# One score product per query tile for the query tiles with one or two key blocks: all four heads of a group in one pair of PSUM banks

## What is computed

```python
x = x + 0.5 * ffn(layernorm(x))     # 8 experts, top 2 of them, 128 -> 512 -> 128, exact GELU
x = x + attention(layernorm(x))     # 16 heads of 64, one shared K and V head
x = x + 0.5 * ffn(layernorm(x))
```

```python
q = (x @ Wq) split into 16 heads, times 64 ** -0.5;  k, v = x @ Wkv   # k, v: one head for all
sim = q @ k.T + rel_emb[bucket(distance)] * 8.0
sim = where(key > query, -max, sim)                                    # causal
out = softmax(sim) @ v;  out @ Wout + bout
```

## Time and profile before

| what | value |
|---|---|
| median of 3 runs | 1161.58 us (1161.24 to 1164.48) |
| the profiled execution's own time | 1159.88 us |
| its span, first to last instruction | 1157.9 us |
| mean granted clock of PE | 0.938 |
| PE busy | 949.3 us, 82% |
| DVE busy | 755.4 us, 65% |
| POOL busy | 623.1 us, 54% |
| ACT busy | 603.8 us, 52% |

### The profile page before, as it was taken

One profiled execution on the slowest core, in us unless ns is written; L12 is line 12 of the kernel. 1 busy time (PEld: TensorE's weight loads), 2 busy tenths in 40 slices (PEclk: granted clock), 3 DMA queues, 4 the chain that ended last, 5 costly groups with the idle time before them and its releaser, 6 DMA issues.

```text
span 1157.9 us, 25233 instructions
## 1 busy us (share of the span) xinstructions
PE 949.3 (82%) x7670; PEld 771.9 (67%) x7670; DVE 755.4 (65%) x2652; ACT 603.8 (52%) x1627; POOL 623.1 (54%) x578
## 2 busy tenths in 40 slices
PE   1514999935989999899999899999898881999970
PEld 1514999934666767667777667776676661999970
DVE  4682222226898788978788897778878865333327
ACT  1201333314867777767788768777577661333320
POOL 2153445437677873448745559654486552455543
PEclk9996999976999999999999999999999995999995
DMA  7898888831457775200000000000000001777646
GB/s 206 127 99 256 209 211 208 200 82 44 72 90 124 126 123 105 39 5 32 4 2 2 1 13 27 2 2 1 2 29 11 1 20 51 209 204 210 202 135 198
DMA packets 105951, 106.57 MB, mean 92 GB/s; under 512 B 10034, under 2 KB 77748, under 8 KB 105824
## 3 DMA queue, kind: packets, MB, share of 16 engines
q1 hardware_dynamic: 96720, 86.41, 31.6%
q0 software_dynamic: 9104, 18.57, 7.2%
HBM read 65.22 MB, written 40.24 MB: 91 GB/s over the span
## 4 chain that ended last, share of the span: by engine, by line
PE 58%; DVE 19%; issue 7%; DMA 7%; SPq 3%; POOL 2%; ACT 2%; another core or an unknown queue 1%; DVEq 1%; POOLq 0%; ACTq 0%
PE bank L1431 11%; PE bank L1363 9%; PE bank L1440 9%; PE bank L1373 9%; PE bank L1456 8%; PE bank L1463 4%; DMA yg<-y_dram,pos_row 2%; DVE prob L1253 2%; DVE pT L1266 1%; PE bank L1296 1%; DMA xr<-slot_dram 1%; PE bank L1298 1%; PE bank L1297 1%; DVE x_sb L1131 1%; POOL yg L762 1%
## 5 line engine op out<-in xcount | busy, mean ns | idle before, releaser
L789 POOL TENSOR_TENSOR prob<-prob,rsum 128x256 f32<-128x256 f32 (+3 forms) x256 | 315.1, 1257 | 214.0 <-DVE rsum L1260 213.4
L874 ACT ACTIVATE prob<-prob,negmax 128x384 f32<-128x384 f32 (+3 forms) x512 | 282.4, 553 | 102.8 <-DVE negmax L1253 101.8
L1253 DVE CUSTOM_DVE_ANT_0 prob<-bank,bias_tab 128x384 f32<-128x384 f32 (+3 forms) x512 | 232.5, 484 | 55.5 <-PE bank L1431 52.6
L834 ACT ACTIVATE hT<-bank 128x512 f32<-128x512 f32 x144 | 86.0, 597 | 255.4 <-PE bank L1363 255.4
L1431 PE MATMUL bank<-kst,qst 64*128 64x256 f32 (+2 forms) x1536 | 182.4, 356 | 29.0 <-DVE negmax L1253 13.3
L1440 PE MATMUL bank<-ident,prob 128*128 128x128 f32 x1280 | 185.6, 279 | 3.4 <-ACT pT L881 3.2
L1431 PEld LDWEIGHTS bank<-kst,qst 64*128 64x128 f32 x1536 | 118.8, 191 | 86.4 <-issue 50.5
L1440 PEld LDWEIGHTS bank<-ident,prob 128*128 128x128 f32 x1280 | 145.2, 142 | 35.5 <-issue 17.3
L1120 DVE COPY yo<-bank 128x128 f32<-128x128 f32 x144 | 42.0, 291 | 194.0 <-PE bank L1373 181.5
L1456 PE MATMUL bank<-pT,vst 128*64 128x256 f32 x1280 | 165.5, 393 | 1.0 <-DVE pT L1266 0.9
L1363 PE MATMUL bank<-xrT,w1t 128*128 128x128 f32 x1152 | 155.0, 278 | 2.9 <-DMA w1t<-L_ffn_fc_w 2.3
(11 more groups left out here) (213 smaller groups left out, 1157.3 us busy)
## 6 DMA issues: line engine op xcount, KB each, us to landing
w1t<-L_ffn_fc_w SPq DMA_DIRECT2D x144, 256.0 KB
slot_dram<-fill SPq DMA_DIRECT2D x15, 975.0 KB
bias_dram<-hg SPq DMA_DIRECT2D x1, 5120.0 KB, 54.7
xr<-slot_dram SPq DMA_DIRECT2D x72, 65.0 KB
y_dram<-yo SPq DMA_DIRECT2D x72, 64.0 KB
bias_tab<-bias_dram SPq DMA_DIRECT2D x1, 4096.0 KB, 13.1
in_tile<-y_dram SPq DMA_DIRECT2D x8, 512.0 KB, 4.7
slot_dram<-fill SPq DMA_DIRECT2D x2, 1040.0 KB
```

Of the source, the lines that this page charges most:

```text
L789: g.tensor_tensor(out=pv, in0=pv, in1=rsum[:, n % 8, hs].unsqueeze(2).to_broadcast([P, 2, (n % QT + 1) * P]), op=ALU.mult).then_inc(norm_d ...
L834: a.activation(hT[:, n % 2, :], bank[2 + n % 2][:], ACT.Gelu).then_inc(gelu_done, 1)
L874: a.activation(prob[n % 8][:, h, :], prob[n % 8][:, h, :], ACT.Exp, scale=-1.0, bias=negmax[:, i % 8:i % 8 + 1], accum_out=lsum[:, n % 8, ...
L1253: v.tensor_tensor_reduce(out=prob[n % 8][:, h, :], in0=BANK_OF["S", b, n, h // 2][h % 2][:, 0:w], in1=bias_tab[:, HG * (n // QT) + h, SEQ ...
```

## The change

For the units with t = 0 or 1 the two S tasks become one, `("S", b, n, 0)`, with twelve matmuls. It takes one pair of front banks: bank o holds head o of pair 0 in its columns 0 to 255 and head o of pair 1 in its columns 256 to 511. Its semaphore counts only when both pairs are done. The TTRs of all four heads wait for it; the TTR of head 2 frees the first bank, that of head 3 the second. It needs the QL of both pairs. Its due time is that of the earlier c = 0 task. Units with t = 2 or 3 stay as they were.

```diff
+        def products(t):
+
+            return [(0, 1)] if t < 2 else [(0,), (1,)]
+
+        def product_of(t, c):
+
+            return 0 if t < 2 else c
...
-                    for c in range(2):
-                        task(("S", b, n, c), {"pe": (0.34, 0.34, 0.5, 0.66)[t]},
-                             [("KL", b), ("QL", b, g, c), ("T", *earlier(b, n, 8), t)], "front", None, 2)
+                    for pairs in products(t):
+                        task(("S", b, n, pairs[0]), {"pe": (0.68, 0.68, 0.5, 0.66)[t]},
+                             [("KL", b), ("T", *earlier(b, n, 8), t)] + [("QL", b, g, c) for c in pairs], "front", None, 2)
                     for h in range(HG):
-                        task(("TTR", b, n, h), {"dve": (0.28, 0.41, 0.55, 0.68)[t]}, [("S", b, n, h // 2), ("EXP", *earlier(b, n, 2), h)],
-                             None, (("S", b, n, h // 2), h % 2))
+                        s_task = ("S", b, n, product_of(t, h // 2))
+                        others = [("TTR", b, n, h - 2)] if len(products(t)) == 1 and h >= 2 else []
+                        task(("TTR", b, n, h), {"dve": (0.28, 0.41, 0.55, 0.68)[t]}, [s_task, ("EXP", *earlier(b, n, 2), h)] + others,
+                             None, (s_task, h % 2) if others or len(products(t)) == 2 else None)
...
-                        w = (n % QT + 1) * P
-                        dve.wait_ge(s_ps, S_PS["S", b, n, h // 2])
+                        t = n % QT
+                        w = (t + 1) * P
+                        c0 = product_of(t, h // 2)
+                        at = max(w, 256) * (h // 2 - c0)
+                        dve.wait_ge(s_ps, S_PS["S", b, n, c0])
...
-                        v.tensor_tensor_reduce(out=prob[n % 8][:, h, :], in0=BANK_OF["S", b, n, h // 2][h % 2][:, 0:w],
+                        v.tensor_tensor_reduce(out=prob[n % 8][:, h, :], in0=BANK_OF["S", b, n, c0][h % 2][:, at:at + w],
...
                         if t == 0:
-                            pe.wait_ge(misc_free, MISC_FREE["QL", b, g, c])
-                        if n == 0 and c == 0:
+                            pe.wait_ge(misc_free, max(MISC_FREE["QL", b, g, c] for c in range(2)))
+                        if n == 0:
                             pe.wait_ge(misc_free, MISC_FREE["KL", b])
-                        for i, (zq, zk) in enumerate(((0, 0), (0, 1), (1, 0))):
-                            for o in range(2):
-                                rows = slice(o * DH, (o + 1) * DH)
-                                ins = t_.matmul(out[o][:, 0:w], qst[rows, g % 2, zq, c, t * P:(t + 1) * P], kst[rows, b % 2, zk, 0:w],
-                                                start=(i == 0), stop=(i == 2))
-                                if i == 2:
-                                    ins.then_inc(s_ps, 1)
+                        pairs = [x for x in products(t) if x[0] == c0][0]
+                        for c in pairs:
+                            at = w * (c - c0)
+                            for i, (zq, zk) in enumerate(((0, 0), (0, 1), (1, 0))):
+                                for o in range(2):
+                                    rows = slice(o * DH, (o + 1) * DH)
+                                    ins = t_.matmul(out[o][:, at:at + w], qst[rows, g % 2, zq, c, t * P:(t + 1) * P], kst[rows, b % 2, zk, 0:w],
+                                                    start=(i == 0), stop=(i == 2))
+                                    if i == 2 and c == pairs[-1]:
+                                        ins.then_inc(s_ps, 1)
```

More of the change, by code:

```diff
@@ L1420, in attention_pe @@
                     elif kind == "S":
-                        _, _, n, c = k
+                        _, _, n, c0 = k
                         g, t = divmod(n, QT)
```

## The result

The changed kernel takes **1151.89 us** (median of 6 runs, 1145.83 to 1153.75) against 1163.1 us for the kernel before (6 runs, 1161.24 to 1165.21). The ratio is **0.9896, interval 0.9877 to 0.9914**: 11.2 us or 1.0% faster. The forecast was 1156.2 in a range of 1147 to 1166. So the time lies in the range, but the gain is twice the 5.4 us that were forecast, and outside the 3.5 to 9 us that the forecast gave itself.

What follows compares the result with a forecast made beforehand. PE was taken to bound the attention, fully in 240 us and partly in 440 us. Terms 2.4 + 4.6 - 1.6 = 5.4 us off the profiled 1159.88 gave 1154.5, plus 1.7 for the median: 1156.2 us, range 1147 to 1166.

Steps and rivals of the forecast that it cites:

- Part 1, visits: PE in attention: joining 29 split units saves 0.25 us of row-form visits each, less ten lost joins with neighbours; 2.4 us faster.
- The factor 0.4: Share of saved PE time assumed felt where PE isn't full, a little over the 33.5% of named PE lines in the chain.
- Part 2, banks: Front banks: merged units take two instead of four, so a quarter of 18.5 us of PE waits goes; 4.6 us faster.
- mixed stretches: The 440 us of 280 to 960 us holding 45.2 us of PE's idle time; PE time saved counts only partly there.
- the same banks' waits before 384- or 512-wide scores instead: Sign of being wrong: PE's waits for front banks would reappear before the wider scores.
- Part 3, later reduces: DVE's reduces of heads 0 and 1 can start 0.35 us later and hold banks longer; 1.6 us slower.
- PE's wait for the second QL: PE's first scores of a group wait for both QLs, 2.7 us before; nothing counted, twice that the worst.
- The idle before scores by negmax: Sign of being right: PE's idle time before scores, waiting for DVE's reduces, would be under 10 us.
- The full stretches within 1 us: Sign of being right: the 240 us where PE idles only 1.4 us would keep their length within 1 us.
- DVE starves: Rival, chance 0.20: later first reduces of merged units are felt where PE isn't full, banks give nothing; 1166.4 us.
- Waits move: Rival, chance 0.25: DVE sets the mixed stretches' length, PE finishes sooner and waits more; only 0.5 us stays, 1161.1 us.
- Banks give more: Rival, chance 0.13: half of both front-bank waits goes, 14.3 us faster in all, 1147.2 us.

Runs made afterwards that it cites:

- e1: Changed kernel, same list, plus one 8-column whole-array matmul between the two pairs of each of the 64 merged units: 1178.9 us, 1.0111 of the kernel before.
- e2: Changed kernel, same list, with the extra 8-column matmul between the pairs in the row form, so no form is left: 1163.2 us, 0.9986 of the kernel before.
- e3: Changed kernel with units' scores in order and merged pairs in four banks, one per head, instead of two: 1188.0 us, 1.0194 of the kernel before.
- e4: Changed kernel, two banks kept, with the added rule that units' scores are made in order: 1145.6 us, 0.9828 of the kernel before.
- e12: e3 with the same list, but the first pair of a merged unit signalled as soon as done: 1198.9 us, 1.0095 of the kernel before, on another chip.
- e7: Changed kernel with the list scheduler's LEAD at 1.07 in place of 1.1: 1141.7 us, 0.9822 of the kernel before.
- e10: Changed kernel with the list scheduler's STAY at 2.0 in place of 1.0: 1143.1 us, 0.9653 of the kernel before.

## Why the prediction was right, and where not

**Right in sign and range; the size was half of what came.** 5.4 us were summed, the medians differ by 11.2. The profiled executions differ by 6.1, but that agreement is luck (which two executions were profiled), and the terms behind it didn't come as they were priced.

- *Part 1, visits (2.4 us)*: **the count was the term that was mis-sized.** 29 splits less ten lost joins make 19 visits; the new list has 35 fewer, since 20 times the units of t = 0 and t = 1 now join in one visit of 24 matmuls. No list without the change has such a visit, and two whole units would have asked for eight of the four front banks. Whether the room or the second pair's earlier due time brings it wasn't tested apart. PE's work at the full clock fell by 8.2 us, 0.23 for each of the 35 visits; the price of 0.25 was about right (0.30 on PE in e1 against e2). *The factor 0.4* was argued from the chain's share of PE lines, which says where the chain ran and not what PE time is worth. e1 and e2 put it at 0.5 to 0.8. With 35 visits it would have mattered: the sum took 2.4 us where 35 x 0.25 is 8.8 in full.
- *Part 2, banks (4.6 us)*: the waits for front banks did fall, by more than that: those of the prediction's 18.5 us to 11.3 + 1.9 + 1.5 + 1.3 = 16.0, those for B2, of which nothing was taken, from 8.6 to 3.9. But PE's idle time fell by only 0.8 us. Waits for kst rose from 1.7 to 6.1 us, those of the routing's transposes for slot from 0.6 to 4.7, of the projection for ot from 1.4 to 3.5. How much of this is the bank term, and how much is PE being done sooner in mixed stretches and waiting (part 1's factor), the totals can't tell apart: 0.8 us is what was left of both. The prediction had named one sign ("the same banks' waits before 384- or 512-wide scores instead"), and it is there: the 256-wide scores have none left and the wide ones 11.2 us. In three other lists idle time fell by 5 to 11 us. e3 shows the worth of the room from the other side: 42 us, near half of it clock.
- *Part 3, later reduces (-1.6 us)*: no loss is seen. DVE's wait for scores fell from 52.6 to 44.6 us. The first reduce does start later (1.05 against 0.71 us after the start of a visit, in the two that are shown).
- *PE's wait for the second QL*: 3.1 us against 2.7, so nothing, as taken, though the 3.1 just passes the "over 3 us" that was named as a sign of being wrong.
- *A term that wasn't in the sum*: the clock. Nothing was taken for it, and in these lists it moves the gain of the attention by -1.8 to 13.0 us, more than any term that was in it.
- *The other signs*: only groups of twelve or more, and the same count of matmuls, came. The idle before scores by negmax was to be under 10 us and is 11.3. "The full stretches within 1 us" was wrong: matched by work they are 5.6 us longer, and the mixed ones give more than the whole gain.
- *Rivals*: "DVE starves" is refuted by DVE's waits. Its threshold in the prediction doesn't follow: by its own numbers (0.35 us a unit, against 2.4 us) the change turns to a loss once 7 of the 41 are felt, and to one of over 3.5 us at 17, not at a third of them. "Waits move" is half true: the waits for banks went to other partners, but the time is far from the 1161.1 that it named. "Banks give more" named 14.3 us, and 11.2 lies nearer to it than to 5.4, but the idle time that it rests on isn't in this pair. The Trainium skill (PSUM — Partial Sum Buffer, Summary: rules for kernel authors) asks that what is read while a matmul runs lie in a different bank; the changed kernel keeps to this by making all reduces wait for the twelve matmuls. The later first reduce above is its price, and in this trace it doesn't show as a loss.

Of the 11.2 us, 5.1 are not in the profiled pair. The spread of the runs is as large: the changed kernel's six runs differ by 7.9 us and the clock between fastest and slowest by 0.006, of 1152 us 6.9.

Still open: what in a list decides how often the clock falls, whether sharing the banks itself keeps it up or the lists without the change were unlucky in it, and how the waits won at the banks come back elsewhere in the list as given.

## What to carry to other kernels

Price a change of the array's form from start to start of neighbouring groups, a quarter of a microsecond for a visit here. Where TensorE is not full, count half of it to most of it (0.5 to 0.8 here), not the share of its lines in the chain. Count the visits in the new list before you price them: the new order joined units that the old one kept apart. Where several short products share a few PSUM banks, fill a bank with two of them before taking another: a bank for each cost 3.7% (e3 against e4), and an earlier start of the reader in those four banks got back about 1%, measured across two chips (e12). With an order made by a scheduler one list is one sample: compare a change under several settings before its size is believed, and split the result in work, clock and idle time; here the same change gave 1.0, 1.5, 2.3 and 2.5%, and about half of what set them apart was clock. Three of the versions (e4 at 0.983, e7 at 0.982 and e10 at 0.965 of the kernel before beside them) beat both kernels of the case.

## What was unexpected of the hardware

A float32 matmul of 8 columns, which the trace shows as two matmuls with a weight load each, costs 0.16 us in the row form among others of that form (e2 against the changed kernel). The granted clock fell from 1.00 to 0.5 in short pieces all through the attention: seven times before the change, each time behind an idle gap of PE of 0.6 to 2.8 us, while other gaps of over 1.5 us brought no fall. Lists with less idle time mostly had less of it: 42.5 us idle and 34.1 us at the lower level before, 34.7 and 16.6 in e4, 56.2 and 62.4 in e3. It is no rule, though: e1 had the least idle time, 32.1 us, and 41.2 us at the lower level. And the kernel before took 2% more on one chip than on the others. Whether the other kernels of that set did so too can't be said, since they ran on that chip only.
